# Two transposes of a graph kernel moved from TensorE to a DMA trip with 32x32 VectorE transposes

## What is computed

```
h = max(layernorm(x), 0)
q, k, v = h Wq', h Wk', h Wv'
rel = adj.T * (q k')                 # 64 x 64 for each graph
rel = rel / norm(rel, axis=2)
x = x + rel v
h = max(layernorm(x), 0)
repeat 3 times:                      # adj stands for in_mat and out_mat
    a = adj h ;  av = concat(a, a)
    z = sigmoid(av w3' + b3 + h u3' + bu3)
    r = sigmoid(av w4' + b4 + h u3' + bu3)
    c = tanh(av w5' + b5 + (r * h) u5' + bu5)
    h = (1 - z) * h + z * c
x = x + h
```

## Time and profile before

| | us |
|---|---|
| median of 3 runs | 1008.0 |
| lowest and highest run | 1005.01, 1008.33 |
| the profiled execution | 1006.57 |
| its span, first to last instruction | 1004.8 |
| PE busy | 981.5 (98%) |
| DVE busy | 652.9 (65%) |
| ACT busy | 517.6 (52%) |
| POOL busy | 78.6 (8%) |

### The profile page before, as it was taken

One profiled execution on the slowest core, in us unless ns is written; L12 is line 12 of the kernel. 1 busy time (PEld: TensorE's weight loads), 2 busy tenths in 40 slices (PEclk: granted clock), 3 DMA queues, 4 the chain that ended last, 5 costly groups with the idle time before them and its releaser, 6 DMA issues.

```text
span 1004.8 us, 15262 instructions
## 1 busy us (share of the span) xinstructions
PE 981.5 (98%) x5448; PEld 849.1 (85%) x5448; DVE 652.9 (65%) x1310; ACT 517.6 (52%) x905; POOL 78.6 (8%) x90
## 2 busy tenths in 40 slices
PE   5899999999999999999999999999999999999996
PEld 4788888888888888888888888888888888888885
DVE  4765657756676675767667666676657757576645
ACT  4455554546446464554735546356554556545552
POOL 1210101101020000100001000100001101010000
PEclk9899999999999999999999999999999999999998
DMA  5010000200011000200002000010000100000001
GB/s 163 1 42 1 1 1 22 63 0 0 0 34 50 0 0 0 83 1 0 0 15 68 0 0 0 21 63 0 0 0 21 63 0 0 0 21 21 1 1 42
DMA packets 21377, 20.06 MB, mean 20 GB/s; under 512 B 2160, under 2 KB 21360, under 8 KB 21360
## 3 DMA queue, kind: packets, MB, share of 16 engines
q1 hardware_dynamic: 21360, 19.83, 6.1%
HBM read 11.44 MB, written 8.39 MB: 20 GB/s over the span
## 4 chain that ended last, share of the span: by engine, by line
PE 96%; DVE 1%; ACT 1%; DMA 0%; issue 0%; POOL 0%; SPq 0%; DVEq 0%
PE gate L308 13%; PE gate L310 13%; PE gate L309 13%; PE cand L308 9%; PE cand L310 9%; PE cand L309 9%; PE fea L408 8%; PE tok L401 4%; PE fea L368 3%; PE tok L308 2%; PE tok L309 2%; PE tok L310 2%; PE fea L308 1%; PE fea L309 1%; PE fea L310 1%; PE tok L417 1%
## 5 line engine op out<-in xcount | busy, mean ns | idle before, releaser
L658 ACT ACTIVATE r_s<-gate,b_r 128x512 f32<-128x512 f32 x96 | 65.0, 685 | 94.3 <-PE gate L310 93.6
L804 DVE TENSOR_TENSOR d_s<-c_s,h 128x512 f32<-128x512 f32 x96 | 64.3, 689 | 67.4 <-ACT c_s L677 67.4
L804 DVE TENSOR_TENSOR a_lo<-fea,a_hi 128x512 fp32r<-128x512 f32 x96 | 65.4, 688 | 49.0 <-ACT a_hi L597 49.0
L677 ACT ACTIVATE c_s<-cand,b_c 128x512 f32<-128x512 f32 x96 | 65.1, 687 | 59.7 <-PE cand L310 59.7
L597 ACT ACTIVATE h_hi<-h 128x512 fp32r<-128x512 f32 x64 | 39.5, 633 | 96.6 <-DVE h L916 96.6
L804 DVE TENSOR_TENSOR rh_lo<-rh,rh_hi 128x512 fp32r<-128x512 f32 x96 | 66.6, 734 | 32.7 <-ACT rh_hi L597 30.7
L597 ACT ACTIVATE a_hi<-fea 128x512 fp32r<-128x512 f32 x96 | 57.4, 599 | 54.8 <-PE fea L408 54.8
L922 DVE TENSOR_TENSOR rh<-r_s,h 128x512 f32<-128x512 f32 x96 | 64.8, 688 | 26.7 <-ACT r_s L658 26.7
L308 PE MATMUL gate<-a_hi,W_hi_wz 128*128 128x512 f32 x192 | 79.1, 412 | 0.0
L308 PE MATMUL cand<-a_hi,W_hi_w 128*128 128x512 f32 x192 | 78.9, 411 | 0.0
L308 PE MATMUL cand<-rh_hi,W_hi_u 128*128 128x512 f32 x192 | 77.5, 404 | 0.0
(11 more groups left out here) (112 smaller groups left out, 2291.5 us busy)
## 6 DMA issues: line engine op xcount, KB each, us to landing
x_s<-x SPq DMA_DIRECT2D x16, 512.0 KB, 4.1
out<-o_s SPq DMA_DIRECT2D x16, 512.0 KB, 3.0
z_s<-w_t SPq DMA_DIRECT2D x1, 512.0 KB, 4.4
r_s<-w_t SPq DMA_DIRECT2D x1, 512.0 KB, 5.3
c_s<-w_t SPq DMA_DIRECT2D x1, 512.0 KB, 6.2
rh<-u_t SPq DMA_DIRECT2D x2, 256.0 KB, 6.5
d_s<-wq SPq DMA_DIRECT2D x1, 256.0 KB, 3.7
d_s<-wk SPq DMA_DIRECT2D x1, 256.0 KB, 4.4
```

The costliest lines, as they stand in the source:

```text
L658: nc.scalar.activation(r_s[:, c, :], gate[:, c, :], ACT.Sigmoid, bias=b_r[:, c:c + 1]).then_inc(r_ready, 1)
L677: nc.scalar.activation(c_s[:, c, :], cand[:, c, :], ACT.Tanh, bias=b_c[:, c:c + 1]).then_inc(c_ready, 1)
L804: return nc.vector.tensor_tensor(dst, a, b, ALU.subtract)
```

## The change

**The turned copies.** For the groups of the main loop, `hx` and `h0` are no longer turned by PE. ACT's `normalise` writes them in blocks (the features of a token are laid out as 4 blocks of 4 x 2 x 32). SP writes the tile to a buffer in DRAM with one DMA of 512 KB, waits for it, and reads it back with four DMAs of 128 KB, so that 32-feature blocks stand on the partitions that they belong to. DVE then turns 32x32 blocks, two instructions of 128 x 512 each for a tile (`turn`), into `hxT` or `h`. The high and low parts are split from these SBUF tiles rather than from PSUM. `TOK_ROUND` loses its four entries `split x X`, `split x Y`, `new 5`, `new 0`.

**The plain copy.** `adjacency` of a new group still reads `h0` in plain order; POOL makes this from the blocked tile `h0_blk` with four copies of 128 x 256 (`h0_in_order`), and PE waits for them (`h0_plain`).

**The order.** The queries of X move from the middle of step 2 to behind its `candidate_a`, those of Y from the end of step 3 to the same place in step 4; values come ahead of scores. In steps 5 and 0 both halves of the adjacency stand together ahead of `candidate_a`. On DVE, `turn_hx` stands behind `split_state` in steps 2 and 4, `turn_h0` behind the statistics in step 5 and at the end of step 0. On SP the trips stand between the loads and the stores.

The first pair's groups, and the last round without attention, are as before.

```diff
+            def blocks_back(back, trip, done):
+                for b in range(BL):
+                    sp.dma_start(back[b * K:(b + 1) * K].rearrange("t a x y z -> t a (x y z)"),
+                                 trip.rearrange("(a t) (b x) -> b t a x", t=K, b=BL)[b]).then_inc(done, 16)
+
+            def turn_hx(g, s):
+                sp.wait_ge(hx_ready, Q * (g + 1))
+                sp.dma_start(hx_trip[s], hx[:].rearrange("p q d -> p (q d)")).then_inc(hx_out, 16)
+                sp.wait_ge(hx_out, 16 * (g - 1))
+                blocks_back(hx_back, hx_trip[s], hx_in)
...
                     load_x(2 * i + 2 + s, s)
+                turn_hx(2 * i + 2, 0)
+                turn_hx(2 * i + 3, 1)
+                turn_h0(2 * i + 2, 0)
                 store(2 * i, 0, use_in_round("final 5", i))
+                turn_h0(2 * i + 3, 1)
                 store(2 * i + 1, 1, use_in_round("final 0", i))
...
+            def h0_in_order(g, s):
+                pool.wait_ge(h0_ready, Q * (g + 1))
+                pool.wait_ge(fence_done[3], g - 1)
+                nc.gpsimd.tensor_tensor(fence[:, 4:5], ones[:], ones[:], ALU.mult).then_inc(fence_done[3], 1)
+                for q in range(Q):
+                    last = nc.gpsimd.tensor_copy(h0[s][:, q, :].rearrange("p (c b f) -> p c b f", c=C, b=BL),
+                                                 h0_b[:, :, :, :, q])
+                last.then_inc(h0_plain, 1)
...
                 inverse_std(1, 2 * i + 3)
+                h0_in_order(2 * i + 2, 0)
                 keep_resid(2 * i + 2, 0, use_in_round("final 5", i))
+                h0_in_order(2 * i + 3, 1)
                 keep_resid(2 * i + 3, 1, use_in_round("final 0", i))
...
-                    if attention:
-                        transpose_hx(2 * i + 2, use("split x X"))
                 elif k == 2:
                     pe.wait_ge(h_lo_ready, 8 * i + 2)
                     reset_gate(w, s, use("adj 1"))
-                    if attention:
-                        queries(2 * i + 2, use("q X"), use("split x X"))
...
                     if attention:
+                        queries(2 * i + 2, use("q X"))
+                        values(2 * i + 2, use("v X"))
                         scores(use("rel X"), use("q X"))
-                        values(2 * i + 2, use("v X"))
...
                     if new:
-                        pe.wait_ge(h0_ready, Q * (2 * i + 3))
-                        transpose_new(2 * i + 2, o, use("new 5"))
+                        pe.wait_ge(h0_plain, 2 * i + 1)
                         adjacency(0, h0[o], use("adj 5"))
+                        adjacency(1, h0[o], use("adj 5"))
                     candidate_a(w, s)
-                    if new:
-                        adjacency(1, h0[o], use("adj 5"))
...
+            def turn(dst, back, c):
+                return nc.vector.transpose(dst[:, c, :].rearrange("p (q a t) -> p a q t", q=Q, a=BL), back)
+
+            def turn_hx(g):
+                dve.wait_ge(hx_in, 16 * BL * (g - 1))
+                for c in range(C):
+                    turn(hxT, hx_back[:, :, :, c, :], c).then_inc(hxT_turned, 1)
...
                     if attention:
                         statistics(1, 2 * i + 3, 1, use("sum Y"))
                     if new:
-                        take_new(w + 1, o, use("new 5"))
+                        turn_h0(2 * i + 2, o)
                     split_rh(w)
```

More of the change, by code:

```diff
@@ L106, in gated_graph_kernel @@
         ones = sb("ones", [P, 1])
-        fence = sb("fence", [P, 4])
+        fence = sb("fence", [P, 5])
         minus_half = sb("minus_half", [P, Q])
@@ L202, in gated_graph_kernel @@
         rnorm_ready = sem("rnorm_ready")
-        fence_done = [sem(f"fence_done{n}") for n in range(3)]
+        fence_done = [sem(f"fence_done{n}") for n in range(4)]
         block = ctx.enter_context(nc.Block())
@@ L344, in transpose_hx, with queries @@
                     last.then_inc(tok_full, 1)
-            def queries(g, n, n_hx):
+            def queries(g, n, n_hx=None):
                 pe.wait_ge(hxT_hi_ready, 2 * g + 2)
-                tok_done(n_hx)
+                if n_hx is not None:
+                    tok_done(n_hx)
+                else:
+                    pe.wait_ge(hxT_lo_ready, 2 * g - 2)
                 for c in range(C):
@@ L514, in window @@
                     if attention:
+                        queries(2 * i + 3, use("q Y"))
+                        values(2 * i + 3, use("v Y"))
                         scores(use("rel Y"), use("q Y"))
-                        values(2 * i + 3, use("v Y"))
                     candidate_rh(w, s)
@@ L539, in window @@
                     update_gate(w, s)
-                    pe.wait_ge(h0_ready, Q * (2 * i + 2))
-                    transpose_new(2 * i + 1, o, use("new 0"))
+                    pe.wait_ge(h0_plain, 2 * i)
                     adjacency(0, h0[o], use("adj 0"))
+                    adjacency(1, h0[o], use("adj 0"))
                     candidate_a(w, s)
-                    adjacency(1, h0[o], use("adj 0"))
                     candidate_rh(w, s)
@@ L584, in _ @@
             adjacency(1, h0[1], n("adj 0"))
+            tok_done(n("new 0"))
             with pe.Fori(0, PAIRS - 1) as i:
@@ L652, in split_new @@
                     copy(h_hi[s][:, c, :], tokT[:, c, :]).then_inc(h_hi_ready, 1)
+            def split_new(g, s):
+                for c in range(C):
+                    act.wait_ge(h_new_ready, 2 * g + (c + 1))
+                    copy(h_hi[s][:, c, :], h[s][:, c, :]).then_inc(h_hi_ready, 1)
             def reset_sigmoid(w):
@@ L738, in window @@
                     if new:
-                        split_new(o, use("new 5"))
+                        split_new(2 * i + 2, o)
                     update_sigmoid(w)
@@ L749, in window @@
                     split_rh(w)
-                    split_new(o, use("new 0"))
                     update_sigmoid(w)
@@ L775, in _ @@
             split_v(n("v 1"))
-            split_new(0, n("new first"))
+            split_new_start(0, n("new first"))
             split_S(n("rel 1"))
@@ L788, in _ @@
             update_sigmoid(0)
-            split_new(1, n("new 0"))
+            split_new_start(1, n("new 0"))
             split_a(1, 0, n("adj 0"))
@@ L888, in split_a, with turn_h0, split_new, take_new_start @@
                 sub(a_lo[s][:, c, :], fea[:, c, :], a_hi[s][:, c, :]).then_inc(fea_taken, 1)
-            def take_new(v, s, n):
+            def turn_h0(g, s):
+                dve.wait_ge(h0_in, 16 * BL * (g - 1))
+                for c in range(C):
+                    turn(h[s], h0_back[:, :, :, c, :], c).then_inc(h_new_ready, 1)
+            def split_new(v, s):
+                for c in range(C):
+                    dve.wait_ge(h_hi_ready, 2 * v + (c + 1))
+                    sub(h_lo[s][:, c, :], h[s][:, c, :], h_hi[s][:, c, :]).then_inc(h_lo_new, 1)
+            def take_new_start(v, s, n):
                 for c in range(C):
@@ L1015, in window @@
                     split_rh(w)
-                    take_new(w + 1, o, use("new 0"))
                     split_a(w + 1, o, 0)
                     split_a(w + 1, o, 1)
+                    turn_h0(2 * i + 1, o)
+                    split_new(w + 1, o)
             n = use_in_start
+            dve.sem_inc(h_lo_new, 4)
             statistics(0, 0, 0, 1)
@@ L1051, in _ @@
             mask_scores(n("rel 1"))
-            take_new(0, 0, n("new first"))
+            take_new_start(0, 0, n("new first"))
             split_S(1)
@@ L1071, in _ @@
             split_rh(0)
-            take_new(1, 1, n("new 0"))
+            take_new_start(1, 1, n("new 0"))
             split_a(1, 1, 0)
```

116 lines of the change are left out of this document (75 added, 41 removed).

## The result

| | before | after |
|---|---|---|
| median of the runs, us | 1007.57 | 1038.94 |
| lowest and highest, us | 1005.01, 1008.33 | 1038.62, 1040.71 |
| ratio, 95% interval | | 1.032 (1.0298 to 1.0342) |
| span of the profiled execution, us | 1004.8 | 1038.4 |

The change makes the kernel 3.2% slower, by 31 us. The forecast was 1021.0, 18 us less than that, with a range of 1010 to 1036.

The account below looks back on a forecast made before the run. PE, busy 98% of the span without a gap in its rounds, was taken as the bound. 1006.57 + 2.5 (wait for POOL less saved transposes) + 10.5 (low clock) = 1019.6, plus 1.4 to the median: 1021.0 us, range 1010 to 1036.

Parts of the forecast that it names:

- The bound: Whole round: PE, busy 98% of the span, has no slack, so every wait of PE is added in full.
- What PE loses: Transposes of X and Y, hx and h0: 0.88 us a block, 24.6 us in all; joined adjacency saves nothing.
- The trips and the turns: DRAM trips and DVE turns in steps 2, 4 and ahead of step 1: in time for PE, cost nothing.
- The wait for POOL: Step 5, copies of h0 of X behind Y's power: PE stands still 3.9 us; a round nets +0.36, 2.5 in all.
- I take 1.6, near the slow one: Step 5: POOL's four copies of h0 of X together take 1.6 us, bounded by 1.04 and 3.0.
- The clock: Behind the step 5 gap: a half-clock stretch costs 1.5 us a round, 10.5 us in all; bounds 0 and 3.3 a round.
- The range: Whole kernel: 1010 to 1036 us, meant to leave out no more than 2 in 10.
- All is covered: Rival: no wait for POOL in step 5, the change gives what it removes, 983.4 us; chance 0.06.
- The gap, but the clock stays at 2.4 GHz: Rival: PE waits in step 5 but its clock doesn't fall, 1010.5 us; chance 0.12.
- The trips come late: Rival: four reads back don't overlap, PE waits at step 1 and in step 2, 1035 to 1050 us; chance 0.17.

Follow-up runs that it names:

- e1: The changed kernel with POOL's four copies of h0 of X moved up from step 5 to step 3, behind inverse_std of X: 983.19 us, ratio 0.976.
- e5: The kernel before with only both adjacency halves put together ahead of candidate_a in steps 5 and 0: 1006.93 us, ratio 0.9999.
- e7: e1 with the trip of h0 made 2.6 us longer by a second DMA out: 983.15 us, ratio 0.977.
- e8: e1 with the trip of h0 made 5.2 us longer by two more DMAs out: 994.57 us, ratio 0.989.
- e3: The changed kernel with DVE waiting for h0_plain ahead of split_rh in step 5, so no subtractions run beside POOL's copies of X: 1021.52 us, ratio 1.014.
- e4: The changed kernel with one contiguous POOL copy of 1024 elements in place of the four strided ones, feature order not undone: 1021.9 us, ratio 1.014.
- e2: The changed kernel with 24 added matmuls in front of PE's wait for h0_plain in step 5, filling the gap: 1023.52 us, ratio 1.016.

## Why the prediction was wrong

**The bound: right.** PE without a gap sets the time, each wait of it is added in full, and all of the difference is on PE.

**What PE loses: right.** 0.88 us a block against 0.86 measured in e1; nothing for the joined adjacency against nothing in e5. The Trainium skill's 390 ns for one bf16 transpose ("VectorE: DVE Perf Modes", The three transpose paths) isn't what an f32 one costs in this kernel, 0.11 us in a block of eight. Nor does its advice to leave 128x128 transposes to TensorE where PSUM will do (Rules for kernel authors) hold where TensorE is the bound: e1 without 224 of them is 2.4% faster.

**The trips and the turns: right.** The forecast took 3.0 us out, 5.5 back, and 2.5 to spare for `h0` of Y. Measured: 2.6 out, 1.7 of issue and 2.8 to the last landing, 4.5 back; and 3.5 to 4.0 to spare (e1, e7, e8).

**The wait for POOL: right in place, cause and start; mis-sized in one term.** The step that failed is "I take 1.6, near the slow one", with its bound of 3.0. The four copies take 3.26 us. The copy of the earlier trace rows was one instruction that DVE held up once, by 0.46 us, and the forecast took its 1.51 over to four instructions nearly as it was. Each of the four is held up, by 0.46 us each, and without DVE they take 1.43 (e3, e4). So the gap is 5.7 instead of 3.9 us, and a round loses 2.17 instead of 0.36: 7 x 1.8 = 12.7 us of the 18 that are missing.

**The clock: right at the gap that was forecast.** The forecast took 1.5 us a round, the shorter of the two stretches of the earlier trace rows. Behind gaps of 3.9 to 4.0 us, the length forecast, the runs show 1.5 (e3) and 1.25 (e4), and the time of e4 as a whole is the forecast's, 1021.9 against 1021.0. That the value fits is in part luck: it was read off a stretch in the start of the trace that has nothing to do with this gap. Behind the gap of 5.7 us it is 2.3 (after against e2): 7 x 0.8 = 5.5 us. This second part follows from the first; a sum that prices the clock apart from the gap leaves it out. Together 12.7 + 5.5 = 18.2, and 1021.0 + 18.2 = 1039.2, beside 1038.94 measured; both parts are taken from the runs, so this closes the account and isn't a second forecast. The Trainium skill's figure for modelling ("TensorE: Matmul & The Clock Gate", Part 1), a ramp penalty under 1% of a typical kernel's span, doesn't fit a kernel with a gap in each round: here it is 16 us, 1.5%.

**The range: too narrow above.** The forecast's own bounds multiplied out, copies of 3.0 and 3.3 us of clock, would have given 1021.0 + 9.8 + 12.6 = 1043. The range took 2.2 us and 2.3 us as the top of its own case and ended at 1036, so as to leave out 2 in 10. But a longer copy brings the longer low clock with it, so that both ends come together; and the 3.26 us lie above the bound of 3.0.

**The rivals.** *All is covered* was priced at 983.4 on condition that the copies of X don't stand behind the power of Y. In the kernel as changed this isn't so, and e1 makes it so: 983.19. *The gap, but the clock stays at 2.4 GHz* was priced at 1010.5. The clock falls in every round, and e2, where it doesn't, takes 1023.5: that price had the short copies in it. *The trips come late* needed over 8 us for the four reads; they take 4.5.

## What to carry to other kernels

When work is handed to an engine with little to do, ask what stands ahead of it in that engine's queue, and when that is released: POOL was 8% busy and held up an engine at 98%. Moved in front of a power that isn't ready, the same copies cost nothing; behind it, they cost all that the change gains and 3% more. When such work runs beside another engine's, count how many instructions can be held up, and not only the elements. Where two costs hang on the same gap, its length and the clock behind it, bound them together and not one by one.

## What the runs showed that was not expected

- Four POOL copies of 128 x 256 in runs of 32 take 1.43 us with DVE held back and 3.26 us beside DVE subtractions of two SBUF tiles; one contiguous copy of as many elements takes 1.04 and 1.50. That is 0.46 us for each copy instruction that is held up, short or long.
- A PE wait of 1.5 us out of dense work left the clock at 2.4 GHz in 7 rounds of 7, one of 2.8 us brought 1.2 GHz in 4 of 7, and those of 3.7 (e3), 3.8 (e4) and 5.5 us (after) in every round. 168 matmuls whose results nobody reads, put into the gap, made the kernel 15.4 us faster.
- A 512 KB tile goes to DRAM and comes back in four reads in some 7 us (2.6 out, 4.5 back), and a 32x32 block transpose of 128 x 512 f32 on DVE takes 0.69 us, as long as a copy out of PSUM.
